# Gate and up sums of a SwiGLU FFN as seven block products over two blocks of 512 rows

## What is computed

```python
# x: [2048, 512] float32; n = layernorm(x) is taken anew in each line
x = x + 0.5 * (n @ Q.T + bias)                              # stage 0; Q 512x512, dequantised from 6 bits
x = x + s4_conv_0(n)                                        # stage 1; a Toeplitz product n @ T0
x = x + 0.5 * (n @ Q.T + bias)                              # stage 2
x = x + 0.5 * (silu(n @ W_gate.T) * (n @ W_up.T)) @ W_down.T    # stage 3; 1376 hidden units
x = x + s4_conv_1(n)                                        # stage 4
x = x + 0.5 * (silu(n @ W_gate.T) * (n @ W_up.T)) @ W_down.T    # stage 5
```

## Time and profile before

| | us |
|---|---|
| median of 3 runs | 968.42 |
| the profiled execution | 968.6 |
| its span | 966.8 |
| TensorE busy | 941.0 |
| VectorE busy | 361.5 |
| ScalarE busy | 258.5 |
| GpSimd busy | 189.6 |
| DMA | 21.7 MB, 22 GB/s over the span |

### The profile page before, as it was taken

How to read it: one execution, slowest core, us unless ns; L and a number is a source line. 1 busy time by engine, 2 the same in 40 slices (tenths; PEclk the granted TensorE clock), 3 DMA queues, 4 the chain that set the end, 5 groups by cost and what they waited for, 6 DMA issues and landing times.

```text
span 966.8 us, 12613 instructions
## 1 busy us (share of the span) xinstructions
PE 941.0 (97%) x4376; PEld 771.8 (80%) x4376; DVE 361.5 (37%) x671; ACT 258.5 (27%) x415; POOL 189.6 (20%) x491
## 2 busy tenths in 40 slices
PE   3898999999999999999999999999999999999998
PEld 2675988888888878887888899888888788888886
DVE  6787869722132213221322286221321132223112
ACT  3432765422121212211221244121211122122111
POOL 5974899601000000100010033000000001000000
PEclk9999999999999999999999999999999999999999
DMA  8100333100000000000000000000100010001001
GB/s 311 67 1 0 89 96 89 58 1 1 0 1 1 1 1 0 0 0 0 0 0 0 0 0 1 1 1 1 44 0 1 1 43 0 0 0 44 1 1 43
DMA packets 10799, 21.70 MB, mean 22 GB/s; under 512 B 1040, under 2 KB 1296, under 8 KB 10768
## 3 DMA queue, kind: packets, MB, share of 16 engines
q1 hardware_dynamic: 10768, 21.28, 6.7%
HBM read 17.08 MB, written 4.19 MB: 22 GB/s over the span
## 4 chain that ended last, share of the span: by engine, by line
PE 86%; POOL 2%; DVE 1%; issue 1%; DMA 1%; ACT 1%; POOLq 0%; ACTq 0%; SPq 0%; DVEq 0%
PE acc L1038 8%; PE acc L1040 8%; PE acc L1039 8%; PE front L997 4%; PE front L1008 4%; PE front L1004 4%; PE front L1015 4%; PE front L998 4%; PE front L1009 4%; PE front L1000 4%; PE front L1013 4%; PE front L1010 4%; PE front L999 4%; PE front L1014 4%; PE front L1001 4%; PE front L312 3%
## 5 line engine op out<-in xcount | busy, mean ns | idle before, releaser
L864 DVE TENSOR_TENSOR gated<-front,gated 128x512 f32<-128x512 f32 (+1 forms) x88 | 60.8, 691 | 492.3 <-ACT gated L620 262.1
L620 ACT ACTIVATE gated<-front 128x512 f32<-128x512 f32 (+1 forms) x88 | 52.7, 599 | 493.5 <-PE front L1010 246.7
L288 POOL TENSOR_TENSOR minus_mean<-mean_var,constant_columns 128x1 f32<-128x1 f32 x98 | 25.3, 258 | 606.1 <-DVE mean_var L281 606.1
L1038 PE MATMUL acc<-ffn_w_hi,hidden_hi 128*128 128x512 f32 (+1 forms) x352 | 137.9, 392 | 0.0
L1040 PE MATMUL acc<-ffn_w_hi,hidden_lo 128*128 128x512 f32 (+1 forms) x352 | 137.0, 389 | 0.0
L1039 PE MATMUL acc<-ffn_w_lo,hidden_hi 128*128 128x512 f32 (+1 forms) x352 | 137.0, 389 | 0.0
L869 DVE TENSOR_TENSOR hidden_lo<-gated,hidden_hi 128x512 fp32r<-128x512 f32 (+1 forms) x88 | 60.9, 692 | 52.5 <-ACT hidden_hi L630 52.5
L305 ACT ACTIVATE normalised<-x_rows,minus_mean_rstd,rstd 128x512 f32 (+1 forms) x97 | 78.3, 808 | 4.4 <-POOL minus_mean_rstd L295 4.1
L322 ACT ACTIVATE xt_hi<-front 128x512 fp32r<-128x512 f32 x96 | 54.7, 595 | 89.5 <-PE front L312 89.4
L1040 PEld LDWEIGHTS acc<-ffn_w_hi,hidden_lo 128*128 128x128 f32 (+1 forms) x352 | 66.1, 188 | 14.1
L1039 PEld LDWEIGHTS acc<-ffn_w_lo,hidden_hi 128*128 128x128 f32 (+1 forms) x352 | 66.1, 188 | 14.0
(11 more groups left out here) (148 smaller groups left out, 1654.9 us busy)
## 6 DMA issues: line engine op xcount, KB each, us to landing
gated<-wffn SPq DMA_DIRECT2D x32, 260.0 KB, 2.6
x_rows<-x_in SPq DMA_DIRECT2D x3, 1024.0 KB, 12.8
out<-x_rows SPq DMA_DIRECT2D x3, 1024.0 KB, 4.3
x_rows<-x_in SPq DMA_DIRECT2D x2, 512.0 KB, 6.3
q_raw<-qweight SPq DMA_DIRECT2D x4, 256.0 KB, 8.4
out<-x_rows SPq DMA_DIRECT2D x4, 256.0 KB, 2.1
omega_terms<-omega_in SPq DMA_DIRECT2D x1, 768.0 KB, 10.1
small_tables<-table_in SPq DMA_DIRECT2D x1, 517.0 KB, 10.7
```

What stands on the lines that cost most here:

```text
L1038: T.matmul(acc[r][:], hh, Wh[:m, cols], start=(f == 0), stop=False)
```

## The change

The program is written anew as straight code over a list of items (one item is one tile in one stage) and four *units*. A unit is 8 tiles of one FFN stage, two blocks of 512 rows (even and odd tiles). Units 0 and 1 are stage 3, units 2 and 3 are stage 5.

In a unit, the four sums "gate, up x first, second block", over two halves of the 512 inputs, are a 2x2 by 2x2 block product, and are formed with seven block products M1 to M7 (Winograd's form) of 6 matmuls each, 42 in place of 48. The left operands are the weight blocks A11, A12, A22 and the sums S1 to S4, the right ones the transposed row blocks B11, B21, B22 and sums T1 to T4. The products share two banks of `front` (`sum_of`), and each is read out before its bank is used again: ScalarE copies M1 (`snapshot`), VectorE makes seven additions (`first_gate`, `middle_sums`, `first_hidden`, `second_gate`) whose ends count up `front_read`. The hidden tiles of the first block go down in the same unit half (passes q of the first half), those of the second block are made by GpSimd (`second_hidden`, into `H1`) and go down in 11 passes behind the 11 steps.

The weights no longer stay in SBUF. For each step k (one column tile of one unit) SP loads four raw blocks (512 KB) and for each down pass 256 KB; VectorE forms S1 to S4 (`weight_sums`) and the remainders of the raw blocks (`weight_raw_lo`), ScalarE rounds, GpSimd makes the remainders of the sums (`weight_sum_lo`, 128 x 1024) and of the down weights (`down_weight_lo`). The chunks of before are gone from stages 1 and 2. Row operands are made for pairs of tiles: copies and rounding on ScalarE (`pair_copies`, `sums_hi_step`), four sums and the remainders on VectorE (`pair_sums`, `pair_lows`), remainders of the sums on GpSimd (`sums_lo_step`). The tiles of unit 0 are prepared inside stage 2, those of later units in the second half of the unit before. Stage 4 is embedded in units 1 and 2, one tile in each of steps 2 to 9 (`embedded_products`; no tiles in units 0 and 3). `LN_OF_STEP` says in which step a coming tile is normalised: unit 0: two in each of steps 3 to 6; units 1 and 2: one in each of steps 0 to 7 and two in each of steps 7 to 10.

The diff, cut to its core (`...` marks what is left out):

```diff
+WD_RING = 3
+C11, U2, T_SUM, U3, C22, C21, C12 = range(1, 8)
+        def sum_of(k, product):
+            return front[(7 * k + product) % 2]
...
+        def pair_copies(act, pair):
...
+            nc.scalar.activation(XF[w][:], bank(a)[:, 0:2, :], ACT.Copy).then_inc(pair_copied, 1)
+            nc.scalar.activation(XG[w][:], bank(b)[:, 0:2, :], ACT.Copy).then_inc(pair_copied, 1)
+            nc.scalar.activation(operand(OPh, B11, B21 + 1, s), ...).then_inc(pair_hi, 1)
+            nc.scalar.activation(operand(OPh, B22, B22 + 1, s), ...).then_inc(pair_hi, 1)
+        def pair_sums(dve, pair):
...
+            nc.vector.tensor_tensor(t1, bank(b)[:, 0:2, :], XF[w][:], ALU.subtract).then_inc(pair_step, 1)
+            nc.vector.tensor_tensor(t3, bank(b)[:, 2:4, :], XG[w][:], ALU.subtract).then_inc(pair_step, 1)
+            dve.wait_ge(pair_step, base + 1)
+            nc.vector.tensor_tensor(t2, bank(b)[:, 2:4, :], t1, ALU.subtract).then_inc(pair_step, 1)
+            dve.wait_ge(pair_step, base + 3)
+            nc.vector.tensor_tensor(t4, bank(a)[:, 2:4, :], t2, ALU.subtract).then_inc(pair_step, 1)
+        def weight_sums(dve, k):
+            raw = lambda i: flat(Wr, k, i, i + 1)
+            dve.wait_ge(w_in[k % 2], 16 * (k // 2 + 1))
+            nc.vector.tensor_tensor(raw(1 + S1), raw(A21_RAW), raw(1 + A22), ALU.add).then_inc(w_step, 1)
+            nc.vector.tensor_tensor(raw(1 + S3), raw(1 + A11), raw(A21_RAW), ALU.subtract).then_inc(w_step, 1)
+            dve.wait_ge(w_step, 4 * k + 1)
+            nc.vector.tensor_tensor(raw(1 + S2), raw(1 + S1), raw(1 + A11), ALU.subtract).then_inc(w_step, 1)
+            dve.wait_ge(w_step, 4 * k + 3)
+            nc.vector.tensor_tensor(raw(1 + S4), raw(1 + A12), raw(1 + S2), ALU.subtract).then_inc(w_step, 1)
...
+            # SP, step f of unit u
+                    if u or f:
+                        load_down(PASSES * u + f + 2)
+                    load_weights(FT * u + f + 2)
...
+            # GpSimd
+            for u in range(UNITS):
+                for f in range(FT):
+                    k, q = FT * u + f, PASSES * u + f
+                    if f:
+                        second_hidden(k - 1)
+                    down_weight_lo(pool, q + 1)
+                    if k + 1 < STEPS:
+                        weight_sum_lo(pool, k + 1)
+                    for n in LN_OF_STEP[u][f]:
+                        rstd_step(pool, n)
+                second_hidden(FT * u + FT - 1)
+                for j in range(FT):
+                    q = PASSES * u + FT + j
+                    if q + 1 < UNITS * PASSES:
+                        down_weight_lo(pool, q + 1)
+                    if u + 1 < UNITS and j in (0, 2, 4, 6):
+                        sums_lo_step(pool, BLK * (u + 1) + j // 2)
...
+            # ScalarE
+                for f in range(FT):
+                    k, q = FT * u + f, PASSES * u + f
+                    if f:
+                        silu(k - 1, g1, C12)
+                    snapshot(k)
+                    silu(k, g0, C11)
+                    if k + 1 < STEPS:
+                        weight_raw_hi(act, k + 1)
+                        weight_sum_hi(act, k + 1)
+                    down_weight_hi(act, q + 1)
+                    if 1 <= f <= EMBEDDED[u]:
+                        xt_hi_step(act, embedded_item(u, f - 1))
+                    for n in LN_OF_STEP[u][f]:
+                        norm_step(act, n)
+                    act.wait_ge(first_made, k + 1)
+                    hidden_hi(q, g0)
...
+                for j in range(FT):
+                    q = PASSES * u + FT + j
+                    if u + 1 < UNITS and j in (0, 2, 4, 6):
+                        sums_hi_step(act, BLK * (u + 1) + j // 2)
+                    if q + 1 < UNITS * PASSES:
+                        down_weight_hi(act, q + 1)
+                    if u + 1 < UNITS and j in (1, 3, 5):
+                        pair_copies(act, BLK * (u + 1) + (j + 1) // 2)
+                    if j + 1 < FT:
+                        second_hidden_hi(u, j + 1)
...
+            # VectorE
+                for f in range(FT):
+                    k, q = FT * u + f, PASSES * u + f
+                    first_gate(k)
+                    middle_sums(k)
+                    if k + 1 < STEPS:
+                        weight_sums(dve, k + 1)
+                        weight_raw_lo(dve, k + 1)
+                    if f == 0 and u:
+                        for r in range(BLK):
+                            ffn_update(u - 1, 1, r)
+                    if 2 <= f < 2 + EMBEDDED[u]:
+                        update_step(dve, embedded_item(u, f - 2))
+                    for n in LN_OF_STEP[u][f]:
+                        stats_step(dve, n)
+                        aggregate_step(dve, n)
+                    if 1 <= f <= EMBEDDED[u]:
+                        xt_lo_step(dve, embedded_item(u, f - 1))
+                    first_hidden(k)
+                    second_gate(k)
+                    hidden_lo(q, g0)
+                hidden_lo(q1, H1[:, 0, :])
+                if u + 1 < UNITS:
+                    pair_sums(dve, BLK * (u + 1))
+                for r in range(BLK):
+                    ffn_update(u, 0, r)
...
+            # TensorE
+            def product(k, which, a, b):
+                o = sum_of(k, which)[:]
+                for j in range(2):
+                    wh, wl = Wh[:, k % 2, a, j, :], Wl[:, k % 2, 1 + a, j, :]
+                    xh, xl = OPh[:, b, j, :], OPl[:, b, j, :]
+                    T.matmul(o, wh, xh, start=(j == 0), stop=False)
+                    T.matmul(o, wh, xl, start=False, stop=False)
+                    last = T.matmul(o, wl, xh, start=False, stop=(j == 1))
+                last.then_inc(m_ready, 1)
+                    pe.wait_ge(w_raw_ready, k + 1)
+                    if k:
+                        pe.wait_ge(front_read, READS * (k - 1) + C21)
+                    product(k, M1, A11, B11)
+                    if k:
+                        pe.wait_ge(front_read, READS * (k - 1) + C12)
+                    product(k, M2, A12, B21)
+                    pe.wait_ge(w_sum_ready, k + 1)
+                    pe.wait_ge(snap_done, k + 1)
+                    product(k, M6, S2, T2)
+                    pe.wait_ge(front_read, READS * k + C11)
+                    product(k, M5, S1, T1)
+                    pe.wait_ge(front_read, READS * k + U2)
+                    product(k, M7, S3, T3)
+                    if 2 <= f < 2 + EMBEDDED[u]:
+                        embedded_products(embedded_item(u, f - 2))
+                    down(q - 1, ALL)
+                    if 1 <= f <= EMBEDDED[u]:
+                        embedded_transposes(embedded_item(u, f - 1))
+                    pe.wait_ge(front_read, READS * k + T_SUM)
+                    product(k, M4, A22, T4N)
+                    pe.wait_ge(front_read, READS * k + C22)
+                    product(k, M3, S4, B22)
+                for j in range(-1, FT - 1):
+                    if u + 1 < UNITS and j in PAIR_BEFORE_PASS:
+                        pair_transposes(BLK * (u + 1) + PAIR_BEFORE_PASS[j])
+                    down(PASSES * u + FT + j, ALL)
```

More of the change, by code:

```diff
@@ L18 @@
 from contextlib import ExitStack
+from dataclasses import dataclass
 import numpy as np
@@ new lines, in pair_items, with is_light, tp_bank @@
+def pair_items(pair):
+    u, s = pair // BLK, pair % BLK
+    if u == 0:
+        return [n for n in range(PRE) if ITEMS[n].kind == "prep" and ITEMS[n].number // 2 == pair]
+    n = UNIT_ITEMS[u - 1] + EMBEDDED[u - 1] + 2 * s
+    return [n, n + 1]
+def is_light(n):
+    return ITEMS[n].kind != "prep"
+def tp_bank(n):
+    if n < PRE:
+        return n % 4
+    if is_light(n):
+        return 2
+    s, i = (ITEMS[n].number % UTILES) // 2, ITEMS[n].number % 2
+    return (2 if s % 2 == 0 else 0) + i
@@ L426, in _ @@
             TT(nal, inv, minus, ALU.mult).then_inc(coef_ready, 1)
-            for t in range(SLOTS):
-                rstd_step(pool, 0, t, t)
+            for n in range(XT_SLOTS):
+                rstd_step(pool, n)
             for j in range(KT):
@@ L512, in _ @@
[L512 to L525 removed]
+                if n in range(4, 4 + KT):
+                    invert(n - 4)
@@ new lines, in _, with add, first_gate @@
+                if n == PRE - 5:
+                    weight_raw_lo(dve, 0)
+            def add(k, product, read, out, other):
+                dve.wait_ge(m_ready, 7 * k + product)
+                assert read in (C11, U2, T_SUM, U3, C22, C21, C12)
+                V.tensor_tensor(out, sum_of(k, product)[:], other, ALU.add).then_inc(front_read, 1)
+            def first_gate(k):
+                dve.wait_ge(snap_done, k + 1)
+                if k:
+                    dve.wait_ge(hid_ready, (k - 1) // FT * PASSES + (k - 1) % FT + 1)
+                add(k, M2, C11, g0, m1)
+                add(k, M6, U2, u2, m1)
@@ L890, in _ @@
+            for r in range(BLK):
+                ffn_update(UNITS - 1, 1, r)
```

(1 more changed line is left out.)

1060 lines of the change are left out of this document (573 added, 487 removed).

## The result

The changed kernel takes 1071.16 us (median of 4 runs, 1070.26 to 1072.82) against 968.41: ratio 1.106, 95% interval 1.104 to 1.108. The forecast was 1063. The profiled execution took 1071.23 at a span of 1069.4.

A forecast was written before the change was run, and what follows sets the result against it. Program order across VectorE, ScalarE and GpSimd was taken to bind the changed kernel: 190 + 780.4 - 60.5 - 1.8 + 153.7 = 1061.8 us span, 1063 forecast (chance 0.48). Range: 1023 to 1128 around the forecast, 1000 to 1125 with the shorter chain.

The forecast's parts named there:

- start 190: Stages ahead of the units: the first unit was let start at 190 us, 3.7 later than the first block before.
- matmuls and transposes 718.1: TensorE's work from the units' start: 780.4 us before, less 60.5 for 264 matmuls and 1.8 for moved transposes.
- waits 153.7: TensorE's waits in the units: 42.6 us in unit 0, 49.1 each in units 1 and 2, 12.9 in unit 3.
- 46 us against TensorE's 39.4: Last 20 items ahead of the units: GpSimd's summed work, 46 us, set against TensorE's 39.4.
- Plain steps: Steps without norm or embedded tile: the chain makes M7 readable at 13.4 us against TensorE's 12.4, 1.0 lost.
- two passes with a pair: Second hidden half: VectorE, ScalarE and GpSimd follow one another for 8.4 us where passes and transposes need 6.4.
- The exclusion: VectorE with two SBUF inputs and GpSimd reading SBUF exclude one another; holds cost about 0.55 us each, 25 in all.
- The clock: Rival, chance 0.20: TensorE's pauses halve its clock, about 1.5 us in each of 26 norm steps, some +40, 1105 us.
- Code fetch at nothing: Straight code instead of loops: TensorE's issue waits could add 0 to 30 us; taken as 0, covered by other waits.
- The weights by DMA at nothing: Weight loads in every unit cost nothing: issued at a step's end, needed over 10 us later; down weights fit two passes.
- TensorE stays the bound (914): Rival, chance 0.13: GpSimd and ScalarE run a step ahead, waits shrink to some 5 us, total 914.
- U3 and C22, then the four block sums: VectorE's order in a step after M7 is readable: these take 2.97 us, then ScalarE rounds the sums, done at 4.08.

The follow-up runs named there:

- number 9: Number 6 with weight_raw_lo directly behind the block sums on VectorE and weight_sum_lo ahead of down_weight_lo on GpSimd: 945.18 us (0.977).
- Number 5: Changed kernel with sums_lo_step (low parts of the row sums) moved from GpSimd to VectorE, ahead of the units and in second halves: 1065.84 us (1.100).
- numbers 11: Number 9 with updates and second-half sums_lo_step reordered on VectorE, plus sums_lo_step on VectorE ahead of the units and pairs behind items 7, 9, 11, 13: 925.10 us (0.956).
- number 12: Numbers 11 with aggregate_step earlier, pair_lows behind the second hidden_lo, and second_hidden_hi ahead of the last norms and pair_copies: 914.11 us (0.944).
- number 7: Changed kernel with the gate product reading one factor from an unused PSUM bank instead of SBUF, in unit 3 alone: 1065.31 us, one execution.
- number 6: Changed kernel with norms behind the next snapshot, block sums earlier, and second-half sums_hi_step behind down weights and next hidden_hi on ScalarE: 958.12 us (0.991).
- numbers 2 and 3: Each against the changed kernel: first, block sums left out, raw blocks loaded instead, 979.57 us, one execution; second, same sums earlier, behind U2, 989.08 us (1.022).

## Why the prediction was right, and where it was not

**The sum.** Forecast: start 190, matmuls and transposes 718.1, waits 153.7. Measured: start 201.3, the same 718.1 of work, and 150.0 besides, of which 16.0 are the clock's and 134 are waits. With 0.229 a matmul a unit's own work is 169.8 us (188.6 with eight embedded tiles); the distances of the snapshots, 211.3, 236.9 and 237.3, leave 41.5, 48.3 and 48.7 (forecast 42.6, 49.1, 49.1), and 11.5 are left for unit 3 (12.9). So three terms were off: +11.3, +16.0 and -20. That they partly cancelled, and left the forecast 8 us off, is luck; the mechanism does not rest on it. The line between work and waits depends on the 0.229 besides. That spacing came from steps of the kernel before; at the 0.227 of number 9's plain steps the 2904 matmuls of the units are 7 us less, and the waits 141.

**The start (190, was 201.3).** Stage 1 and the step into stage 2 shrank by 7.1 us where 5.3 were estimated (first update of stage 2 at 133.2, 140.31 before). The 190 was besides rounded down: its own terms add up to 191.2 (186.4 - 5.3 + 3.5 + 6.6). The term that failed is "46 us against TensorE's 39.4": I compared sums of engine time. The chain that ended last shows a loop of 8.9 us for each pair instead:

```profile
172.60 2.36 POOL row_operands_lo L516
174.96 1.22 POOL x_rows L689
...
177.46 0.82 ACT normalised L433
...
179.63 0.80 ACT normalised L433
180.44 0.95 ACT row_operands_hi L512
181.46 2.38 POOL row_operands_lo L516
```

GpSimd's row lows, its bias addition, the norm behind its `rstd_step`, ScalarE's next norm, ScalarE's rounding of the pair sums that stands behind it, and the lows again. It runs from 172.60 to 181.46, and GpSimd's next lows start at 190.49. I had read orders inside a step and sums of time ahead of the units; it needed the orders in both. Number 5, which takes only the lows out of this loop, started the units 4.2 us earlier; numbers 11 and 12, which change engine, place and order there, 6.4 and 8.7.

**The waits (153.7, were 134).** In the rows above all links are 0.2 to 0.3 us early, and 0.22 of that stems from the first one, VectorE's reads and block sums (2.75, priced at 2.97); the links behind it were right within 0.1. Plain steps lost 0.6 and not 1.0 (0.8 at 0.227 a matmul); two passes with a pair took 7.8 and not 8.4. Steps with one norm came out at 16.7 (16.8), with three at 19.0 (19.3), with two at 17.8 where the clock held (18.0).

**The exclusion** was priced right: the held product ends 0.55 behind GpSimd's instruction, and number 7 shows the hold to be a link of the plain step. The 25 us for all holds were not measured as a whole. **The clock** was costed at nothing, with a rival at 1.5 us in each of 26 steps. The price was right (1.6), the count was not: 10 stretches. The answer lay between forecast and rival. **Code fetch at nothing** was right. The waits put down to issue ahead of products, 69.8 us in the row above, would have spoken against it; but with the same number of instructions they are 8.5 in number 6:

```profile
PEld front L1294 <- issue: 8.5, 10, 2.2
```

They were the shadow of other waits. In number 12 none of the waits listed for TensorE in the units is put down to issue. **The weights by DMA at nothing** was right too: ScalarE waits 41.1 us in all for down weights to land in the changed kernel, but 35.9 in number 12 as well, where TensorE's listed waits in the units are 3.2 us in all.

**TensorE stays the bound (914)** did not happen in the changed kernel. Other orders get there: number 12 measured 914.11, with a start at 192.6 in place of 190.

**What the prediction missed** is how much the sums' place weighs. It has "U3 and C22, then the four block sums", and prices the sums; that ScalarE and GpSimd wait for M7's read, which they don't need, for 3 us, stands in no term. It showed only when numbers 2 and 3 were set side by side.

## What to carry to other kernels

Matmuls saved are time only while every other engine's queue lets TensorE run on. Sums of busy time do not show that (here VectorE was busy for 69% and GpSimd for 47%): lay out one step with each engine's instructions in program order, and count a wait for all that stands behind it. Where such a chain binds, move independent work behind what TensorE waits for before anything is made cheaper; here order, with one kind of low part moved to another engine, was worth 157 us, where the removed matmuls are 60.5.

## What the runs showed of the hardware that was not expected

- The holds between VectorE and GpSimd go both ways: `weight_raw_lo` 1.96 and `weight_sum_lo` 3.06 us when their queues meet, 0.97 and 2.41 when they don't.
- The same pause of about 2.5 us ahead of M6 was followed by 3 us at half clock in some steps (19.4 and 19.5 us) and not in others (17.8). Six matmuls in the pause made it none of four in unit 0. What decides it between steps stays open.
- Two stops of 0.1 us between matmuls, too short to be listed as waits, were 0.20 of the 0.23 us that a plain step of number 6 lost.
